# Cross-attention of a decoder layer at both of its ends: earlier prompt loads, shared copies, biases through TensorE, a changed order of routing and adding transfers

## Time and profile before

| | |
|---|---|
| median of 3 runs | 1404.74 us |
| profiled execution, its own time | 1410.6 us |
| its span in the profile | 1408.8 us |
| mean granted clock of TensorE | 0.941 |
| busy share TensorE, VectorE, ScalarE, GpSimd | 91%, 61%, 58%, 54% |
| stages on TensorE | set-up to 141, self-attention to 657, cross-attention 665 to 919, experts from 952 |

### The profile page before, as it was taken

The page is one execution under the profiler, slowest core; times in us unless marked ns, Lnnn a source line. Parts: engine busy times, 40 slices in busy tenths (PEclk is TensorE's granted clock), DMA queues, the critical chain, the costliest instruction groups (busy, mean ns, idle before and its releaser), DMA issues.

```text
span 1408.8 us, 19065 instructions
## 1 busy us (share of the span) xinstructions
PE 1286.5 (91%) x6219; PEld 553.9 (39%) x6219; DVE 854.9 (61%) x1483; ACT 816.3 (58%) x957; POOL 766.6 (54%) x513
## 2 busy tenths in 40 slices
PE   8987899999999999997999998909999999999990
PEld 3543122222222222222345444505666666666650
DVE  3443788888888888885257656443444444444444
ACT  4544799999999999995665545402222222222224
POOL 2223577777777777775265675452444444444433
PEclk9999899999999999999899989558999999999995
DMA  6599444485558434443366944491222222222227
GB/s 220 158 322 262 192 69 69 68 252 84 81 88 241 69 68 69 73 81 117 105 149 152 206 126 136 122 235 30 46 46 47 47 47 46 48 47 46 46 31 246
DMA packets 114698, 161.63 MB, mean 115 GB/s; under 512 B 29281, under 2 KB 78214, under 8 KB 114278
## 3 DMA queue, kind: packets, MB, share of 16 engines
q1 hardware_dynamic: 89488, 120.55, 33.6%
q0 software_dynamic: 24992, 39.74, 15.3%
q10 hardware_dynamic: 118, 0.05, 0.0%
HBM read 108.07 MB, written 52.76 MB: 114 GB/s over the span
## 4 chain that ended last, share of the span: by engine, by line
PE 82%; DMA 4%; DVE 4%; SPq 3%; ACT 3%; issue 2%; another core or an unknown queue 1%; POOL 1%; POOLq 0%; ACTq 0%; DVEq 0%
PE xp_ps_h L2264 18%; PE sa_o L646 17%; PE sa_sum L632 13%; PE xp_ps_y L2282 8%; PE sa_factor L632 5%; PE qp_ps L312 3%; PE cb_l L1228 2%; PE cb_att L1240 2%; PE xp_ps_g L2272 2%; PE cb_misc L1215 2%; PE cb_misc L1195 1%; SPq L232 1%; PE cb_misc L1270 1%; PE xp_ps_x L2254 1%
## 5 line engine op out<-in xcount | busy, mean ns | idle before, releaser
L679 DVE TENSOR_TENSOR sa_probs<-sa_sum,sa_strips 128x1024 f32<-128x1024 f32 x352 | 413.3, 1219 | 74.2 <-PE sa_sum L632 70.0
L723 POOL TENSOR_TENSOR sa_probs<-sa_probs,sa_factors 128x1024 f32<-128x1024 f32 x160 | 381.1, 2382 | 133.9 <-ACT sa_probs L697 133.9
L703 ACT ACTIVATE sa_probs<-sa_probs 128x1024 f32<-128x1024 f32 (+1 forms) x256 | 341.2, 1373 | 0.3 <-DVE sa_probs L679 0.3
L646 PE MATMUL sa_o<-sa_probs,sa_v 128*17 128x512 f32 x2048 | 270.2, 600 | 1.1 <-POOL sa_probs L723 0.5
L2264 PE MATMUL xp_ps_h<-big,arena 128*128 x568 | 257.9, 597 | 1.3 <-ACT arena L2317 1.1
L2234 POOL DMA_INDIRECT y_sum<-stage,xp_place_of x71 | 112.2, 1581 | 216.3 <-DVE stage L2371 200.0
L632 PE MATMUL sa_sum<-sa_q,sa_k 97*128 97x512 bf16 x704 | 199.3, 387 | 6.0 <-DVE sa_k L517 4.2
L2317 ACT ACTIVATE arena<-xp_ps_x 128x256 f32<-128x256 f32 x71 | 27.2, 383 | 306.3 <-PE xp_ps_x L2254 306.3
L697 ACT ACTIVATE sa_probs<-sa_factor 128x1024 f32<-128x1024 f32 x160 | 163.2, 1020 | 27.0 <-PE sa_factor L632 27.0
L2264 PEld LDWEIGHTS xp_ps_h<-big,arena 128*128 128x128 f32 x568 | 108.6, 192 | 108.9 <-issue 105.4
L632 PEld LDWEIGHTS sa_sum<-sa_q,sa_k 97*128 97x128 bf16 x704 | 48.6, 98 | 251.0 <-DVE sa_probs L679 195.1
(11 more groups left out here) (231 smaller groups left out, 1391.3 us busy)
## 6 DMA issues: line engine op xcount, KB each, us to landing
sa_q<-qstack SPq DMA_DIRECT2D x96, 128.0 KB
sa_k<-kstack SPq DMA_DIRECT2D x96, 128.0 KB
sa_strips<-line SPq DMA_DIRECT2D x3, 3840.0 KB, 14.8
oT<-sa_o_out SPq DMA_DIRECT2D x32, 256.0 KB, 2.3
kstack<-qp_parts SPq DMA_DIRECT2D x48, 128.0 KB, 3.0
qstack<-qp_parts SPq DMA_DIRECT2D x48, 128.0 KB
sa_factors<-factor_line SPq DMA_DIRECT2D x3, 1920.0 KB, 18.9
vpad<-qp_v_out SPq DMA_DIRECT2D x16, 272.0 KB, 2.9
```

What stands on the lines that cost most here:

```text
L646: last = nc.tensor.matmul(ps_o[n % 2][32 * h:32 * h + VW, :], v[m % 2][:, jt, VW * h:VW * (h + 1)], probs[s % RING][:, h, :], start=(jt == ...
L679: nc.vector.tensor_tensor(probs[s % RING][:, 2 * half:2 * half + 2, :], ps_sum[sums_before(s, half) % 2][:, :, :], strips[hg % 2][:, 2 * h ...
L703: nc.scalar.activation(probs[s % RING][:, 0:heads, :], probs[s % RING][:, 0:heads, :], ACT.Exp, scale=0.25).then_inc(exp_done, 1)
L723: nc.gpsimd.tensor_tensor(probs[s % RING][:, 2:4, :], probs[s % RING][:, 2:4, :], factors[hg % 2][:, :, c1 - CH:c1][:, :, ::-1], ALU.mult) ...
```

## The change

Loads and copies at the head of the cross stage:

- Chunk 0's loads are issued at n = 27 (behind batch 1's denominators), and the factors of the low-rank products at n = 29, into the storage of the even head groups' keys and queries. `q` and `k` become two halves of one tile for that.
- The reciprocals move from step 13 to step 10 of a batch's sixteen.
- VectorE copies the odd low-rank products, ScalarE the even ones. Both engines wait for the last `oT` stores themselves. `root1(0)` goes ahead of `scale(1)` on GpSimd.

At its end:

- In chunk 7 `turn_x2(6)` goes ahead of the logits 6 and 7, `gate(6)` ahead of the outputs 2, and `low_rank2(0)`, `(1)`, `(2)` in between; the others follow, all ahead of `turn_x2(7)`.
- VectorE does `choose_experts(6)` ahead of chunk 7's divide and `place_rows(6)` behind its statistics; the check takes three columns.
- W2's transfers are four of 1 MB, in the order q, i = (1, 0), (0, 0), (0, 1), (1, 1), and all ahead of the last scatter.
- The biases are loaded as rows of 8 experts (4 x 16 KB, into `stage`) and spread by TensorE with a column of the identity as stationary operand; ScalarE copies them.
- The flag is set ahead of `place_rows(7)` and the tables; GpSimd and TensorE wait for a new semaphore `tables_made` at the start of the experts.

```diff
@@ attention_space
+    pairs = {i: sb(f"qk{i}", [P, 2 * half]) for i in (1, 0)}
...
+        "f13": [pairs[0][:, F13_AT + n * 3 * KT * D:F13_AT + (n + 1) * 3 * KT * D].rearrange("p (q c) -> p q c", q=2)
+                for n in range(2)],
@@ self_attention, sync
+                store_output(sp, io, sa, n)
+                if n == NSTEP // JT - 1 - IH:
+                    for w, name in enumerate(("factors1", "factors3")):
+                        sp.dma_start(sa["f13"][w], io[name].rearrange("q p c -> p q c")).then_inc(sa["f13_loaded"], 16)
...
                     sp.dma_start(cc["den"][:, b, :], den_rows(io, b)).then_inc(cc["den_loaded"], 16)
+                    if b == 1:
+                        sp.wait_ge(cc["rec_stored"], 16)
+                        load_outputs(sp, io, cc["oc0"], cc["recb0"], 0, cc["oc0_loaded"])
+                        load_residual(sp, io, cc["x10"], 0, cc["x10_loaded"])
                     sp.wait_ge(cc["rec_done"], b + 1)
                     sp.dma_start(rec_rows(io, b), cc["rec"][:, b, :]).then_inc(cc["rec_stored"], 16)
-                if n == NSTEP // JT - 2:
-                    sp.wait_ge(cc["rec_stored"], 16 * (B - 1))
-                    load_outputs(sp, io, cc["oc0"], cc["recb0"], 0, cc["oc0_loaded"])
-                    load_residual(sp, io, cc["x10"], 0, cc["x10_loaded"])
@@ self_attention, vector
-                if hg == HG - 1 and s % STEPS == STEPS - 3 and s // STEPS % B >= 1:
+                if hg == HG - 1 and s % STEPS == JT + 2 and s // STEPS % B >= 1:
@@ cross_block, sync
             sp.wait_ge(sa["pv_done"], NSTEP)
-            for n, name in enumerate(("factors1", "factors3")):
-                sp.dma_start(f13[n], io[name].rearrange("q p c -> p q c")).then_inc(f13_loaded, 16)
...
+            for r in range(4):
+                sp.dma_start(stage[32 * r:32 * r + E_, 0:HID],
+                             bass.AP(io["b13"].tensor, r % 2 * HID, [[2 * HID, E_], [1, HID]])).then_inc(b13_loaded, 16)
...
-            for e in range(5):
-                load_bias(e)
             keep_x2(5)
-            sp.wait_ge(l_filled, LOW + PAIRS * NCH)
-            load_bias(5)
-            sp.wait_ge(normed2, TT * NCH)
-            load_bias(6)
-            wait_filled(sp, "gate", NCH - 1, 0)
-            load_bias(7)
@@ cross_block, tensor
                 if u >= 2:
-                    pe.wait_ge(exp_done, u - 1)
+                    pe.wait_ge((exp_done, low_copied)[u % 2], u // 2)
...
+            def bias(e):
+                if e == 0:
+                    pe.wait_ge(b13_loaded, 64)
+                pe.wait_ge(late_copied, 8 + e - 1)
+                for half in range(2):
+                    at = 32 * (2 * (e % 2) + half)
+                    last = nc.tensor.matmul(ps_l[e % 2][:, half, :], ident[at:at + E_, at + e:at + e + 1].to_broadcast([E_, P]),
+                                            stage[at:at + E_, 0:HID], start=True, stop=True)
+                last.then_inc(late_filled, 1)
...
+            low_rank2(3)
+            ranks(NCH - 2)
+            for u in range(4, 8):
                 low_rank2(u)
             turn_x2(NCH - 1)
-            ranks(NCH - 2)
             gate(NCH - 1)
-            for u in range(5, 8):
-                low_rank2(u)
...
             ranks(NCH - 1)
+            for e in range(E_):
+                bias(e)
@@ cross_block, scalar
+            for u in range(3):
+                copy_w2(u)
+            exp_gap(NCH - 2)
+            for u in range(3, 8):
+                copy_w2(u)
             copy_x2(NCH - 1)
...
+            for e in range(E_):
+                act.wait_ge(late_filled, 8 + e + 1)
...
+                nc.scalar.activation(b13[:, e, :, :], ps_l[e % 2][:, :, :], ACT.Copy).then_inc(late_copied, 1)
@@ cross_block, vector
+            copy_low(1)
+            last1 = statistics1(0)
+            copy_low(3)
+            moments1(0, last1)
+            copy_low(5)
+            copy_low(7)
+            for i in range(2):
+                dve.wait_ge(sa["o_stored"][i], 16 * NSTEP // JT // 2)
             normalise_masked(0)
+            for u in range(9, LOW, 2):
+                copy_low(u)
...
+            dve.wait_ge(dve_done, few_at)
+            nc.vector.tensor_scalar(cc["flag"][:, :], few[:, :], P - 0.5, None, ALU.is_lt).then_inc(ro["flag_set"], 1)
             place_rows(NCH - 1)
             make_tables()
+            dve.sem_inc(ro["tables_made"], 1)
+            dve.wait_ge(late_copied, 8 + E_)
@@ cross_block, gpsimd
             scale(0)
             pool.wait_ge(set_up, 1)
+            root1(0)
             scale(1)
-            root1(0)
...
+            add_w2(0)
+            add_w2(1)
             root2(NCH - 1)
-            add_w2(0)
+            add_w2(2)
             scatter(NCH - 2)
+            add_w2(3)
             scatter(NCH - 1)
-            add_w2(1)
@@ experts
+            pool.wait_ge(ro["tables_made"], 1)
...
+            pe.wait_ge(ro["tables_made"], 1)
```

More of the change, by code:

```diff
@@ L856, in misc_uses @@
         order += [("q", n + 1, k) for k in range(KT) if before]
-    order += [("x2T", NCH - 1, 0), ("x2T", NCH - 1, 1), ("rank", NCH - 2, 0), ("gate", NCH - 1, 0), ("verdict", NCH, 0),
+    order += [("rank", NCH - 2, 0), ("x2T", NCH - 1, 0), ("x2T", NCH - 1, 1), ("gate", NCH - 1, 0), ("verdict", NCH, 0),
               ("rank", NCH - 1, 0)]
@@ L867, in w2_pairs @@
 def w2_pairs():
-    return [(q, i, m) for q in range(2) for i in range(2) for m in range(2)]
+    return [(q, i, m) for q, i in ((1, 0), (0, 0), (0, 1), (1, 1)) for m in range(2)]
 def routing_space(nc, ctx):
@@ L1223, in logits_of @@
                     wait_drained(pe, "q", n, k)
-                if use >= 2:
-                    pe.wait_ge(exp_done, use - 1)
+                if n == 0 and j < 2:
+                    pe.wait_ge((exp_done, low_copied)[j], LOW // 2)
+                else:
+                    pe.wait_ge(exp_done, LOW // 2 + PAIRS * n + j - 1)
                 for h in range(2):
@@ L1336, in _ @@
                 outputs(n, 1)
+                if n == NCH - 1:
+                    turn_x2(n - 1)
                 logits_of(n, 6)
                 logits_of(n, 7)
[L1339 removed]
+                if n == NCH - 1:
+                    gate(n - 1)
+                elif n >= 1:
                     turn_x2(n - 1)
                 outputs(n, 2)
+                if n == NCH - 1:
+                    low_rank2(0)
                 outputs(n, 3)
[L1343 removed]
+                if n == NCH - 1:
+                    low_rank2(1)
+                elif n >= 1:
                     gate(n - 1)
@@ L1618, in _ @@
                     take_gates(n - 1)
+            choose_experts(NCH - 2)
+            nc.vector.reduce_max(worst[:, 0:1], rec[:, :, :].rearrange("p b c -> p (b c)"), AXX)
+            nc.vector.reduce_max(worst[:, 1:2], dinv[:, 0:NTT - TT, :].rearrange("p t h -> p (t h)"), AXX)
             divide(NCH - 1, range(TT))
@@ L1626, in _ @@
             normalise2(NCH - 1)
-            choose_experts(NCH - 2)
-            place_rows(NCH - 2)
             take_gates(NCH - 1)
```

121 lines of the change are left out of this document (65 added, 56 removed).

## The result

The changed kernel runs in 1395.95 us (median of 9 runs, 1387.04 to 1401.65), against 1404.74 (1399.01 to 1408.46, 9 runs) for the kernel before on the same chip. The ratio of the runs is 0.9913, 95% interval 0.9890 to 0.9936: 12.2 us less (9.0 to 15.5 by the interval), where 22.3 were forecast. The two medians themselves lie 8.8 us apart. The profiled execution took 1396.76 us (span 1394.8), 14.0 of span less than the one before.

What follows compares the result with a forecast made beforehand. It took the two seams at the cross stage's ends, late loads and a late first gather, as the bound. Terms +3.0 - 12.3 + 0 + 0.3 - 2.6 - 10.7 = -22.3 took 1404.74 to 1382.4 us, range 1374 to 1393.

Steps and rivals of the forecast that it cites:

- Early reciprocals: Self-attention: reciprocals at step 10 make VectorE wait 1.5 and 2.7 us for denominators; +3 us, bounds 0 to 5.
- the ring: Self-attention: buffering whose slack might swallow VectorE's waits for the denominators, making the loss 0.
- First seam: Self-attention's end to chunk 0's first logits: earlier loads (8.3 us) and shared low-rank copies save 12.3 us, bounds 9 to 14.
- Chunk loop: Cross stage's eight chunks: they keep their pace, bound by TensorE; 0 us, bounds -3 and +3.
- End of stage: Cross stage's end to the tables: reordered gates, choices and low-rank products; +0.3 us, bounds -3 and +4.
- Flag and gather: Second seam, tables to first expert product: early flag saves 2.6 us, earlier adding transfers let the gather land 10.7 sooner.
- Biases: Cross stage's end: bias products and copies, at most 16 us, stay covered before the tables' end; cost 0.
- the step on the adding transfers: Second seam: four 1 MB transfers empty the queue by about 933, saving 10.7 us; GpSimd's fourth issue takes 1.1.
- first seam gives half: Rival: chunk 2's later load or ScalarE's stalls lose 6 to 9 us of the gain; 1390 us, chance 0.14.
- Clock up at the end: Rival: TensorE idles less at the cross stage's end and runs at 2.4 GHz; 1376.4 us, chance 0.13.
- the gather stays late: Rival, second seam: adding transfers and scattered rows slow each other, gather lands 6 us later; 1388.5 us, chance 0.18.
- slower: Rival, chunk loop: moved ScalarE stalls idle TensorE and its clock stays down; 1418 us, chance 0.05.

Runs made afterwards that it cites:

- again: The changed kernel with no edit, profiled a second time; ratio to the kernel before 0.9916, median 1397.94 us.
- adds_late: The changed kernel with the third and fourth 1 MB adding transfers of W2 issued behind the last scatter; ratio to the kernel before 0.9982.
- rec13: The changed kernel with its reciprocals back at step 13 of sixteen; ratio to the kernel before 0.9857, median 1388.95 us.
- late_loads: rec13 with chunk 0's loads back at n = 30 and the factor loads behind the last product; ratio to the kernel before 0.9937.
- one_copier: rec13 with all sixteen low-rank products of w1 and w3 copied by ScalarE; ratio to the kernel before 0.9876.
- low2_late: The changed kernel with w2's low-rank products out of chunk 7, the last three behind the last gate; ratio to the kernel before 0.9984.
- flag_late: rec13 with the flag set behind the routing tables again; ratio to the kernel before 0.9883.
- ranks_late: rec13 with the routing products of chunk n - 2 moved behind the second half of the projection; ratio to the kernel before 0.9962.

## Why the prediction was right in sign and large in size

It forecast 1382.4 with a range of 1374 to 1393. By the ratio the change is worth 12.2 us, which makes 1392.5, half a microsecond inside the range; the changed kernel's median, 1395.95, lies above it. The sum was nearly twice what came. By its steps:

*Early reciprocals: +3, measured +7.5, +7.2 in again.* The mechanism was right (wait for the denominators, 1.5 and 2.7 us forecast, 2.46 and 3.16 in the trace). The size fell outside its bounds of 0 to 5 because the waits were longer, because the step had no term for TensorE's clock, which fell after the second wait (1.6 us), and because it hoped that the ring would swallow part; it swallows none. In adds_late, where the clock stayed up, the loss is 4.6, inside the bounds. Their removal gives 8.3 us by the ratios (rec13).

*First seam: -12.3, measured -9.2, -10.1 in again.* The loads' 8.3 were right (late_loads: 9.5 with the clock). The 4 us for the shared copies failed: one_copier shows them to be worth nothing, or slightly harmful. The step set 2.2 us per pair of products with two copiers against the 2.9 of the trace, and took the difference for the one copier's; but those 2.9 are a mean over 2.25 on the full clock and 3.1 on the slow one (9.39 us for six products from 674.71 on), and with one copier or two a pair takes 2.25 on the full clock. Its "1.02 us at full clock" for a product is a misreading too: the row of 2.04 us has a wait for a copy in it, and two products without one take 1.14 (670.21, before). The walk kept TensorE on the full clock through a chain in which each product waits for a copy, and VectorE's normalising at its old 1.55 us beside a scaling that had moved up to it.

*Chunk loop: 0, measured -8.6 in one profile and +1.2 in the next.* Less half its time at 1.2 GHz it is 173.0 before and 167 to 172 in the nine profiles since, so zero was off by some 3 us in the mean, as far as one profile of before can tell; the bounds of 3 us either way were far too narrow for a single execution.

*End of stage: +0.3, measured +7.2, and +2.3 in again.* From the first logits of chunk 7 to the end of its transposes it takes 27.9 us before (19 of them at 1.2 GHz), 36.4 after (30) and 28.1 in again (11); less half of the slow time, 18.4, 21.4 and 22.6 (about 19 in low2_late, which has no products there). So the three products put 3 to 4 us in front of the last transposes, for which the step had 3; a product unit costs 2.08 us on the slow clock (three of them stand in chunk 7 after), where it had 1.05. From the transposes to the tables it is 37.3 before and 35.7 in nearly every profile since, 1.6 gained. The rest of the +7.2 is the clock of that execution. GpSimd's fourth transfer took 1.72 us where the step on the adding transfers had 1.1.

*Flag and gather: -13.3, measured -12.5, -10.5 in again.* The gather's 10.7 were right: from its issue to TensorE's start it took 13.8 us before and takes 3.1 after, and adds_late shows the cause at its full size. The flag's 2.6 were not: the first gather is issued 3.0 us behind the tables before, 1.3 after and 3.1 in again, since it now waits for the scattered rows to land, and flag_late has it at 2.05 with the flag behind the tables. The term that failed is the "about 0.2" to which the gap was to fall. (935.66 in that step is the flag's end; the tables end at 935.47.)

*Biases: 0.* The last of their copies (1.94 us for two, at 929.77) ends at 931.7, ahead of the tables. Right.

With the means of after and again: +7.3 - 9.7 - 3.7 + 4.8 - 11.5 = -12.8, beside 12.2 measured by the ratio. That the loop and the end of the stage nearly cancel in it is luck of two executions. The range was drawn too tight on its better side by its own terms (their better ends add up to 11.0 us, not 8.5); it reached the result by its worse side, for which it had named other causes. (And of the three slices at 8 in the earlier trace rows behind the set-up, two lie in the cross stage, the third, 951 to 986, in the experts.) The rival "first seam gives half" (1390) comes nearest in time, but not in cause: chunks 0 and 1 take 19.6 and 23.0 us (before 20.0 and 23.0), so no late load of chunk 2 shows. "Clock up at the end" did not happen (first `hidden` 5.73 us), nor did "the gather stays late" nor "slower". The signs asked for were met for `project(0, 0)`, the reciprocals' waits, the flag and the gather; "clock full from 655 to 700" was not.

Open: why TensorE's semaphores come 2 to 4 us behind its products' rows in the middle of chunks 3 to 7 on the slower chip and not on the other. Neither the routing products nor, for want of a case on that chip, the gate's exponential could be made out as the cause.

## What to carry to other kernels

Before an instruction is moved ahead in a queue that feeds TensorE, read from the trace when its input lands, and add to the wait what TensorE's clock loses behind it. A transfer in a shared software queue is paid for by whoever is issued next, and a wait in front of it by everything that its engine has queued behind: list both before its place is chosen. Profile the same kernel twice before a stretch that the change doesn't touch is given a cause.

## What had not been expected of the hardware

An idle stretch of TensorE of 1.7 us, in windows in which it is otherwise busy (3.82 of 5 us in the one ahead of the fall), went ahead of over 10 us at 1.2 GHz (ranks_late). VectorE's four instructions of 0.35 us each take 3.15 us beside one GpSimd instruction of 2.34 us that is itself not slowed. The kernel before took 0.9% less on one chip than on the other, with the same code (1394.05 us against 1407.34 and 1406.82), and TensorE's late semaphores are missing from that chip's three profiles.
